# A gather kernel's first adapter, first activations and last output: found, turned and stored another way

## The chip, the cores and the metric

The kernel runs on one core of one Trainium2 chip. The metric is device time in microseconds (us), the median of the runs. TensorE is called PE, VectorE DVE, ScalarE ACT, GpSimd POOL and SyncE SP, as in the profile.

## The reference

128 samples of 64 x 1024 floats pass two layers, each with a residual. Layer one picks one of 16 matrices of 64 x 64 by a sample's index, layer two one of 8 adapters of 1024 x 1024. The inputs draw the second index from 3 to 7, so five adapters are used.

```python
def _L0_cond_ref(x, weights, condition):
    W = weights[condition]
    return jnp.einsum('bct,bcd->bdt', x, W)
def _L1_cond_ref(x, weight, adapter_ids):
    w = weight[adapter_ids]
    return jnp.einsum('bsi,boi->bso', x, w)
x = x + _L0_cond_ref(x, L0_cond_weights, itok_B_0_15)
x = x + _L1_cond_ref(x, L1_cond_weight, itok_B_3_7)
```

## The kernel before

**The arithmetic.** The identity is added to every matrix, so that the residuals come with the products. With x as 64 rows, z = x times the adapter turned over (the big product), and y = the small matrix times z. Each float operand is split in two float32r parts, hi (a copy) and lo (what is left), and a product is hi x hi, lo x hi and hi x lo.

**Slots.** Samples are sorted by adapter on the chip, and two samples of one adapter make a slot of 128 rows; where a group has an odd count, its last slot holds one. DVE works out a table (a row per slot: samples, how many to store, group, small matrices, chunks), which one DMA moves to one partition (`slot_row`, line 329), where every engine looks fields up (`look`, lines 188 to 195). `groups_ready` tells that POOL has made `group_row`, the adapters in order of their groups (lines 257 to 272).

**Order in a slot.** PE makes the first half of z (`sum_z`, lines 421 to 434, 24 matmuls of 512 columns in a slot of two samples), then y of the slot before (`sum_y`, 6 matmuls), then the second half of z. ACT copies out the hi parts, DVE makes the lo parts, ACT copies y out of PSUM and stores it on its own DMA queue (`store_y`). SP issues all loads. The next adapter comes in chunks during the slots and is turned by DVE; loops run over pairs of slots. There are 66 slots here (line 536 runs 66 times for each of two banks).

**The start.** Before slot 0 all of the first adapter is needed: 8 chunks of 128 x 1024. Chunk c is loaded by SP (`load_first`), gets its identity from POOL (`add_1_to_first`, line 254), is turned by PE in 8 transposes into a pair of PSUM banks (line 411; three pairs in turn), and is kept as hi by ACT (line 511) and lo by DVE (line 691). Chunks 6 and 7 land in the buffers of chunks 0 and 1, once these are turned. x of slot 0 comes in 8 small DMAs (line 343), is turned by DVE in 32 x 32 blocks (line 715), and split (lines 524, 724). POOL adds the identity to the small matrices too (line 275), for ACT and DVE to split (lines 506, 754).

**The end.** After the last z there is nothing left to overlap with: ACT keeps z's second half as hi (536), DVE makes its lo (740), PE sums y (444 to 446), ACT copies it out (541) and stores it (548).

The order of each engine's work is the order in which its block is written; semaphores hold it back. Some waits that matter here are:

```python
sp.wait_ge(groups_ready, 1)
first_ad = sp.value_load(group_row[0:1, 0:1], min_val=0, max_val=NAD - 1)
...
pool.wait_ge(table_moved, 16)
```

Of the kernel before, what the change touches and what calls it, by code (L numbers as in the profile page):

```python
# [5 lines left out]
P = 128  # L6
# [12 lines left out]
def conditional_residual_kernel(nc, x, cond_ids, adapter_ids, cond_w, adapter_w, out):  # L19
# [29 lines left out]
    x_quarters = x.rearrange("n (b r) (a m) -> n a r b m", a=BLOCKS, r=BLOCK)  # L49
    out_rows = out.rearrange("b c t -> (b c) t")  # L50
# [4 lines left out]
    with ExitStack() as ctx:  # L55
# [40 lines left out]

# [30 lines left out]
        group_id = sb("group_id", [1, NAD])  # L128
        group_row = sb("group_row", [1, NAD], I32)
# [23 lines left out]
        x_loaded = [sem(f"x_loaded{h}") for h in range(2)]  # L153
        first_loaded = [sem(f"first_loaded{c}") for c in range(CHUNKS_PER_GROUP)]
# [22 lines left out]
        y_made = sem("y_made")  # L177
        all_done = sem("all_done")
# [40 lines left out]

        block = ctx.enter_context(nc.Block())  # L220
# [5 lines left out]
        def _(pool):  # L226
# [23 lines left out]
            def add_1_to_first(c):  # L250
# [5 lines left out]

            pool.wait_ge(groups_made, 1)
# [48 lines left out]
        def _(sp):  # L306
# [18 lines left out]
            for c in range(2):  # L325
                load_first(c)
# [3 lines left out]
            for c in range(2, 5):  # L330
                load_first(c)
# [54 lines left out]

            for h in range(2):
# [6 lines left out]
        def _(pe):  # L394
# [74 lines left out]
            for c in range(CHUNKS_PER_GROUP):  # L469
                turn_first(c)  # L470
# [332 lines left out]
```

## Time and profile before

| | |
|---|---|
| median of 3 runs | 835.26 us (834.72 to 836.27) |
| the profiled execution | 834.99 us |
| its span | 833.2 us |
| PE busy | 808.3 us, 97% of the span |
| DVE, ACT, POOL busy | 449.6, 280.6, 27.4 us |
| moved over the span | 90.87 MB, mean 109 GB/s |

The profile shows one execution. Busy time is the time in which an engine had an instruction under way; an average over the span says nothing about a short stage at one end of it. A timeline row gives start, duration, engine, source line, what is written and read, how often (x), and in brackets how long the engine had been idle and what released it. SPq and ACTq are the DMA issues of SP and ACT.

### The profile page before, as it was taken

The numbers are of one execution on the slowest core, as the hardware profiler recorded it, in microseconds if no ns is written. First come the engines' busy times: TensorE is split into PE (matmuls) and PEld (weight loads), VectorE is DVE, ScalarE is ACT, GpSimd is POOL, SyncE is SP. The second block draws the span as 40 slices with busy tenths as digits, with TensorE's granted clock in tenths as the row PEclk, the third lists the DMA queues.
The fourth block names the chain that finished last, engine by engine and source line by source line (L and its number), as shares of the span: only waits on it lengthen the run. The fifth ranks groups of instructions, "written<-read, shape, count | busy, mean of one in ns | idle before, by whom it ended". The sixth has DMA issues, their size and how long they took to land.

```text
span 833.2 us, 17872 instructions
## 1 busy us (share of the span) xinstructions
PE 808.3 (97%) x3572; PEld 668.5 (80%) x3573; DVE 449.6 (54%) x466; ACT 280.6 (34%) x515; POOL 27.4 (3%) x61
## 2 busy tenths in 40 slices
PE   3899999999999999999999999999999999999996
PEld 2688888888888888888888888888888888888885
DVE  5756676466665434676663466665443344344432
ACT  2423334342433223333432333333332332232232
POOL 3000000000000000000000000000000000000000
PEclk9899999999999999999999999999999999999999
DMA  4544443444433324444332434433332232233232
GB/s 140 167 125 134 144 140 85 121 123 147 123 104 101 88 72 126 130 142 126 110 101 81 121 122 142 134 102 91 97 100 67 76 101 79 72 101 90 74 88 76
DMA packets 74271, 90.87 MB, mean 109 GB/s; under 512 B 13844, under 2 KB 65044, under 8 KB 74260
## 3 DMA queue, kind: packets, MB, share of 16 engines
q1 hardware_dynamic: 64020, 57.19, 22.3%
q10 hardware_dynamic: 10240, 33.56, 15.3%
q8 instruction: 4, 0.07, 0.0%
q14 instruction: 7, 0.06, 0.0%
HBM read 57.15 MB, written 33.55 MB: 109 GB/s over the span
## 4 chain that ended last, share of the span: by engine, by line
PE 96%; DMA 1%; DVE 1%; issue 1%; SPq 1%; ACTq 0%; POOL 0%; POOLq 0%; ACT 0%; DVEq 0%
PE z_ps L431 14%; PE first_ps L431 14%; PE z_ps L430 14%; PE first_ps L430 14%; PE z_ps L433 14%; PE first_ps L433 13%; PE y_ps L445 4%; PE y_ps L446 4%; PE y_ps L444 4%; DMA w_nat<-in_L_cond_weight_dram 1%; SPq L343 0%; DMA slot_row<-table_i 0%; DMA ids_i<-in_itok_B_dram 0%; PE first_ps L411 0%; ACTq L192 0%
## 5 line engine op out<-in xcount | busy, mean ns | idle before, releaser
L430 PE MATMUL z_ps<-w_hi,xt_hi 128*128 (+1 forms) x528 | 205.5, 389 | 0.0
L431 PE MATMUL z_ps<-w_lo,xt_hi 128*128 (+1 forms) x528 | 205.4, 389 | 0.0
L430 PE MATMUL first_ps<-w_hi,xt_hi 128*128 x528 | 205.4, 389 | 0.0
L431 PE MATMUL first_ps<-w_lo,xt_hi 128*128 x528 | 205.4, 389 | 0.0
L433 PE MATMUL z_ps<-w_hi,xt_lo 128*128 (+1 forms) x512 | 199.2, 389 | 0.0
L433 PE MATMUL first_ps<-w_hi,xt_lo 128*128 x480 | 186.7, 389 | 0.0
L715 DVE STREAM_TRANSPOSE x_turned<-x_in 128x1024 f32<-128x1024 f32 x67 | 143.6, 2143 | 23.9 <-issue 19.5
L524 ACT ACTIVATE xt_hi<-x_turned 128x1024 fp32r<-128x1024 f32 x67 | 71.1, 1061 | 227.7 <-DVE x_turned L715 227.7
L724 DVE TENSOR_TENSOR xt_lo<-x_turned,xt_hi 128x1024 fp32r<-128x1024 f32 x62 | 76.1, 1228 | 77.8 <-ACT xt_hi L524 77.8
L430 PEld LDWEIGHTS z_ps<-w_hi,xt_hi 128*128 128x128 f32 x528 | 99.2, 188 | 20.9
L430 PEld LDWEIGHTS first_ps<-w_hi,xt_hi 128*128 128x128 f32 x528 | 99.1, 188 | 20.8
L431 PEld LDWEIGHTS first_ps<-w_lo,xt_hi 128*128 128x128 f32 x528 | 99.1, 188 | 20.6
L431 PEld LDWEIGHTS z_ps<-w_lo,xt_hi 128*128 128x128 f32 x528 | 99.1, 188 | 20.5
L433 PEld LDWEIGHTS z_ps<-w_hi,xt_lo 128*128 128x128 f32 x512 | 96.1, 188 | 19.8
L433 PEld LDWEIGHTS first_ps<-w_hi,xt_lo 128*128 128x128 f32 x480 | 90.1, 188 | 18.5
L740 DVE TENSOR_TENSOR z_lo<-first_ps,z_hi 128x512 fp32r<-128x512 f32 x66 | 45.5, 689 | 94.8 <-ACT z_hi L536 94.5
L740 DVE TENSOR_TENSOR z_lo<-z_ps,z_hi 128x512 fp32r<-128x512 f32 x66 | 45.5, 689 | 92.4 <-ACT z_hi L536 91.0
L710 DVE TENSOR_TENSOR w_lo<-w_turned,w_hi x32 | 39.4, 1232 | 69.9 <-ACT w_hi L520 69.9
L520 ACT ACTIVATE w_hi<-w_turned x32 | 34.0, 1062 | 122.2 <-DVE w_turned L700 122.2
L541 ACT ACTIVATE y<-y_ps 128x512 f32<-128x512 f32 x132 | 71.3, 597 | 2.1 <-PE y_ps L446 2.1
L536 ACT ACTIVATE z_hi<-first_ps 128x512 fp32r<-128x512 f32 x66 | 39.1, 592 | 90.8 <-PE first_ps L433 66.2
L536 ACT ACTIVATE z_hi<-z_ps 128x512 fp32r<-128x512 f32 x66 | 39.1, 592 | 88.5 <-PE z_ps L433 70.9
(119 smaller groups left out, 444.0 us busy)
## 6 DMA issues: line engine op xcount, KB each, us to landing
x_in<-in_x_dram SPq DMA_DIRECT2D x544, 64.0 KB, 2.0
out_dram<-y ACTq DMA_DIRECT2D x128, 256.0 KB, 3.1
w_nat<-in_L_cond_weight_dram SPq DMA_DIRECT2D x128, 128.0 KB
w_nat<-in_L_cond_weight_dram SPq DMA_DIRECT2D x4, 512.0 KB, 4.3
w_turned<-in_L_cond_weight_dram SPq DMA_DIRECT2D x2, 512.0 KB, 3.8
y<-in_L_cond_weight_dram SPq DMA_DIRECT2D x2, 512.0 KB, 5.1
x_turned<-in_L_cond_weights_dram SPq DMA_DIRECT2D x2, 256.0 KB, 3.9
ids_i<-in_itok_B_dram SPq DMA_DIRECT2D x2, 0.5 KB, 2.1
```

The costliest lines, as they stand in the source:

```text
L430: nc.tensor.matmul(to, xt_hi[h][:, t, :], whi, start=(t == 0), stop=False)
L431: mm = nc.tensor.matmul(to, xt_hi[h][:, t, :], wlo, start=False, stop=last and not pair)
L433: mm = nc.tensor.matmul(to, xt_lo[h][:, t, :], whi, start=False, stop=last)
L444: nc.tensor.matmul(to, w0_slot[:, 0], z_hi[:, n], start=True, stop=False)
L520: nc.scalar.activation(of_chunk(w_hi, k), turned(k), ACT.Copy).then_inc(chunk_hi_made, 1)
L524: nc.scalar.activation(xt_hi[h][:], x_turned[h][:], ACT.Copy).then_inc(xt_hi_made, 1)
L536: nc.scalar.activation(z_hi[:, n], z_banks[h][n][:], ACT.Copy).then_inc(z_hi_made, 1)
L541: nc.scalar.activation(y[h][:, n * HALF:(n + 1) * HALF], y_ps[n][:], ACT.Copy).then_inc(y_made, 1)
L710: nc.vector.tensor_tensor(of_chunk(w_lo, k), turned(k), of_chunk(w_hi, k).bitcast(F32), ALU.subtract).then_inc(chunk_lo_made, 1)
L715: nc.vector.transpose(x_turned[h][:].rearrange("p t (b m) -> p b t m", m=BLOCK), x_in[h][:].rearrange("p (b m t) -> p b t m", b=BLOCKS, m= ...
L724: nc.vector.tensor_tensor(xt_lo[h][:], x_turned[h][:], xt_hi[h][:].bitcast(F32), ALU.subtract).then_inc(xt_lo_made, 1)
L740: nc.vector.tensor_tensor(z_lo[:, n], z_banks[h][n][:], z_hi[:, n].bitcast(F32), ALU.subtract).then_inc(z_lo_made, 1)
```

## The change

- **The first adapter.** DVE multiplies a countdown 8, 7, ..., 1 with "this adapter is used", takes the largest value and subtracts it from 8: the number of the first adapter used, right after the counts are known. SP waits for that (`first_known`) in place of `groups_ready`, and issues six chunks at once, then the table's DMA. The making of `group_row` moves back, to DVE behind the table and to POOL between chunks 3 and 4.
- **x of slot 0.** SP reads the two samples from the table's first row where DVE made it, and loads each with one DMA of 64 x 1024, behind six chunks and the table. PE turns it between chunks 3 and 4, ACT and DVE split it out of PSUM. Chunks 6 and 7 come behind it.
- **The small matrices** get their identity from DVE, ahead of its wait for `gathered`; their lo part is made behind all of the adapter.
- **The last y.** PE takes z_lo last in each half. ACT copies the left half of y, DVE the right one, and SP and ACT each store one sample in two halves of 512 columns.
- **Stores of the other slots** are issued by ACT ahead of the copy of z's second half (`keep_z_hi(s, h, 1)`), where they stood behind it.

```diff
+    x_rows = x.rearrange("b c t -> (b c) t")
...
+        X0 = "x of slot 0"
+        TURN_ORDER = [0, 1, 2, 3, X0, 4, 5, 6, 7]
+        TURN_OF = {what: i for i, what in enumerate(TURN_ORDER)}
+        FOR_FIRST_HALF = 5
...
+        def store_last(eng, k, pairs_past):
+            s = 2 * pairs_past + 1
+            *samples, stores = look(eng, s, SAMPLE_A, SAMPLE_B, STORES)
+            rows = slice(k * C, (k + 1) * C)
+            to = out_rows[bass.ds(samples[k] * C, C), :]
+            with eng.If(stores > k):
+                eng.wait_ge(y_made, 4 * pairs_past + 3)
+                eng.dma_start(to[:, 0:HALF], y[1][rows, 0:HALF]).then_inc(last_stored, 16)
+                eng.wait_ge(last_half_made, 1)
+                eng.dma_start(to[:, HALF:T], y[1][rows, HALF:T]).then_inc(last_stored, 16)
+            with eng.Else():
+                eng.sem_inc(last_stored, 32)
...
+            for c in range(3):
+                add_1_to_first(c)
+            pool.wait_ge(table_moved, 16)
+            nc.gpsimd.tensor_copy(slot_row[:, 1:LOOKED_UP + 1, CHUNKS_BEFORE], slot_row[:, 0:LOOKED_UP, CHUNKS]
+                                  ).then_inc(table_ready, 1)
+            add_1_to_first(3)
...
-            pool.wait_ge(w0_loaded, 2 * 16)
-            nc.gpsimd.tensor_tensor(w0_nat, w0_nat,
-                                    two_ident[:].rearrange("p (n d) -> p n d", n=1).to_broadcast([P, NCOND, C]),
-                                    ALU.add).then_inc(w0_with_1, 1)
-            for c in range(2):
-                add_1_to_first(c)
-            pool.wait_ge(table_moved, 16)
-            nc.gpsimd.tensor_copy(slot_row[:, 1:LOOKED_UP + 1, CHUNKS_BEFORE], slot_row[:, 0:LOOKED_UP, CHUNKS]
-                                  ).then_inc(table_ready, 1)
-            for c in range(2, CHUNKS_PER_GROUP):
+            for c in range(4, CHUNKS_PER_GROUP):
...
-            sp.wait_ge(groups_ready, 1)
-            first_ad = sp.value_load(group_row[0:1, 0:1], min_val=0, max_val=NAD - 1)
+            sp.wait_ge(first_known, 1)
+            first_ad = sp.value_load(first_row[0:1, 0:1], min_val=0, max_val=NAD - 1)
             def load_first(c):
                 if c >= OWN_PLACE:
-                    sp.wait_ge(first_turned, NH * (c - OWN_PLACE) + NH)
+                    sp.wait_ge(first_turned, NH * TURN_OF[c - OWN_PLACE] + NH)
                 sp.dma_start(first_nat[c], adapter_rows[bass.ds((first_ad * CHUNKS_PER_GROUP + c) * P, P), :]
                              ).then_inc(first_loaded[c], 16)
-            for c in range(2):
+            for c in range(6):
                 load_first(c)
             sp.wait_ge(table_made, 1)
             sp.dma_start(slot_row[:, 1:LOOKED_UP + 1, :], table_i[0:LOOKED_UP]).then_inc(table_moved, 16)
-            for c in range(2, 5):
+            _, first_samples = nc.values_load_multi_w_load_instructions(
+                table_i[0:1, SAMPLE_A:SAMPLE_B + 1], engines=[sp.engine], min_val=0, max_val=B - 1,
+                skip_runtime_bounds_check_because="the table is made on the chip, of clipped indices")
+            for k, sample in enumerate(first_samples):
+                sp.dma_start(x_in[0][k * C:(k + 1) * C, :], x_rows[bass.ds(sample * C, C), :]).then_inc(x0_loaded, 16)
+            for c in range(6, CHUNKS_PER_GROUP):
...
-            load_x(0, 0)
-            for c in range(5, CHUNKS_PER_GROUP):
-                load_first(c)
             load_x(1, 1)
-            sp.wait_ge(first_turned, NH * CHUNKS_PER_GROUP)
+            sp.wait_ge(groups_ready, 1)
+            sp.wait_ge(first_turned, NH * len(TURN_ORDER))
+            sp.sem_inc(x_loaded[0], PER_X)
...
+            store_last(sp, 0, pairs_past)
...
-            def turn_first(c):
-                pe.wait_ge(first_with_1, c + 1)
+            def turn_first(i):
+                if TURN_ORDER[i] == X0:
+                    pe.wait_ge(x0_loaded, 32)
+                    nat = x_in[0][:]
+                else:
+                    pe.wait_ge(first_with_1, TURN_ORDER[i] + 1)
+                    nat = first_nat[TURN_ORDER[i]]
...
-                pe.wait_ge(xt_lo_made, 1)
-                pe.wait_ge(first_lo_made, NH * TPB)
+                pe.wait_ge(first_lo_made, NH * FOR_FIRST_HALF)
...
-                sum_y(2 * pairs_past + 1, pair)
+                s = 2 * pairs_past + 1
+                for k in range(2):
+                    pe.wait_ge(w0_placed[k], s + 1)
+                w0_slot, rows = (w0_parts, P) if pair else (w0_twice, C)
+                for n in range(NH):
+                    to = y_ps[n][0:rows]
+                    pe.wait_ge(z_hi_made, NH * s + n + 1)
+                    nc.tensor.matmul(to, w0_slot[:, 0], z_hi[:, n], start=True, stop=False)
+                    nc.tensor.matmul(to, w0_slot[:, 1], z_hi[:, n], start=False, stop=False)
+                    pe.wait_ge(z_lo_made, NH * s + n + 1)
+                    nc.tensor.matmul(to, w0_slot[:, 0], z_lo[:, n], start=False, stop=True).then_inc(y_summed, 1)
...
                 place_w0_a(s)
+                store_y(before, 1 - h)
                 keep_z_hi(s, h, 1)
-                store_y(before, 1 - h)
-            for c in range(4):
-                keep_first_hi(c)
-            keep_xt_hi(0, 0)
-            for c in range(4, CHUNKS_PER_GROUP):
-                keep_first_hi(c)
+            for i in range(len(TURN_ORDER)):
+                keep_first_hi(i)
+            act.sem_inc(xt_hi_made, 1)
...
-            make_y(2 * pairs_past + 1, 1)
-            store_y(2 * pairs_past + 1, 1)
+            act.wait_ge(y_summed, 4 * pairs_past + 3)
+            nc.scalar.activation(y[1][:, 0:HALF], y_ps[0][:], ACT.Copy).then_inc(y_made, 1)
+            store_last(act, 1, pairs_past)
...
+            nc.vector.tensor_scalar(countdown[:], col_i[0:1, 0:NAD], -1.0, float(NAD), ALU.mult, ALU.add)
...
+            link(nc.vector.tensor_scalar(cnt[:, 1, :], counts_ps, 1.0, None, ALU.min))
+            link(nc.vector.tensor_tensor(countdown_used[:], countdown[:], cnt[0:1, 1, :], ALU.mult))
+            link(nc.vector.tensor_reduce(first_from_end[:], countdown_used[:], AX_X, ALU.max))
+            nc.vector.tensor_scalar(first_row[:], first_from_end[:], -1.0, float(NAD), ALU.mult, ALU.add
+                                    ).then_inc(first_known, 1)
             nc.vector.tensor_copy(looked[:, 0, :], ranks_ps)
-            nc.vector.tensor_scalar(cnt[:, 1, :], counts_ps, 1.0, None, ALU.min)
...
+            dve.wait_ge(w0_loaded, 2 * 16)
+            nc.vector.tensor_tensor(w0_nat, w0_nat,
+                                    two_ident[:].rearrange("p (n d) -> p n d", n=1).to_broadcast([P, NCOND, C]),
+                                    ALU.add).then_inc(w0_with_1, 1)
...
+            def keep_x0_lo(i):
+                def keep(samples, to):
+                    for n in range(NH):
+                        at = (slice(None), slice(n * TPB, (n + 1) * TPB), samples)
+                        turned_x = first_banks[i % TURNS][n][:].rearrange("p (t m) -> p t m", t=TPB)[:, :, samples]
+                        dve.wait_ge(first_hi_made, NH * i + n + 1)
+                        nc.vector.tensor_tensor(to[at], turned_x, xt_hi[0][at].bitcast(F32),
+                                                ALU.subtract).then_inc(first_lo_made, 1)
+                stores, = look(dve, 0, STORES)
+                with dve.If(stores > 1):
+                    keep(slice(0, P), xt_lo[0])
+                with dve.Else():
+                    keep(slice(C, P), xt_hi[0])
...
+            for i in range(TURN_OF[X0]):
+                keep_first_lo(i)
+            dve.wait_ge(table_ready, 1)
+            keep_x0_lo(TURN_OF[X0])
+            for i in range(TURN_OF[X0] + 1, len(TURN_ORDER)):
+                keep_first_lo(i)
             dve.wait_ge(w0_hi_made, 1)
             nc.vector.tensor_tensor(w0_all[:, 1], w0_nat, w0_all[:, 0].bitcast(F32), ALU.subtract).then_inc(w0_lo_made, 1)
-            for c in range(4):
-                keep_first_lo(c)
             dve.wait_ge(w0_zeroed, 1)
-            dve.wait_ge(table_ready, 1)
-            turn_x(0, 0)
-            keep_xt_lo(0, 0)
-            for c in range(4, CHUNKS_PER_GROUP):
-                keep_first_lo(c)
-            dve.wait_ge(first_lo_made, NH * CHUNKS_PER_GROUP)
+            dve.wait_ge(first_lo_made, NH * len(TURN_ORDER))
+            dve.sem_inc(x_is_turned, 1)
+            dve.sem_inc(xt_lo_made, 1)
...
+            dve.wait_ge(y_stored[1], 32 * pairs_past + STORED_AHEAD)
+            dve.wait_ge(y_summed, 4 * pairs_past + 4)
+            nc.vector.tensor_copy(y[1][:, HALF:T], y_ps[1][:]).then_inc(last_half_made, 1)
```

POOL's order, from its first wait for data on. `first_loaded` is a chunk's landing, `table_moved` the table's, `groups_made` DVE's part of the groups. Before:

```order
L258 TENSOR_TENSOR used_id<-cnt,col 1x8 [waits groups_made,consts_made]
L260 TENSOR_TENSOR is_group<-is_group,used_id 1x64 [waits pool_step]
L265 TENSOR_TENSOR half_id<-is_group 1x32 [waits pool_step]
L267 TENSOR_TENSOR quarter_id<-half_id 1x16 [waits pool_step]
L269 TENSOR_TENSOR group_id<-quarter_id 1x8 [waits pool_step]
L272 CAST group_row<-group_id 1x8 [waits pool_step]
L275 TENSOR_TENSOR x_turned<-x_turned,two_ident 128x1024 [waits w0_loaded]
L254 TENSOR_TENSOR w_nat<-w_nat,ident 128x128 [waits first_loaded0]
L254 TENSOR_TENSOR w_nat<-w_nat,ident 128x128 [waits first_loaded1]
L282 COPY slot_row<-slot_row 1x70 [waits table_moved]
L254 TENSOR_TENSOR w_turned<-w_turned,ident 128x128 [waits first_loaded2]
```

Now:

```order
L282 TENSOR_TENSOR w_nat<-w_nat,ident 128x128 [waits first_loaded0,consts_made]
L282 TENSOR_TENSOR w_nat<-w_nat,ident 128x128 [waits first_loaded1]
L282 TENSOR_TENSOR w_turned<-w_turned,ident 128x128 [waits first_loaded2]
L288 COPY slot_row<-slot_row 1x70 [waits table_moved]
L282 TENSOR_TENSOR w_turned<-w_turned,ident 128x128 [waits first_loaded3]
L293 TENSOR_TENSOR used_id<-cnt,col 1x8 [waits groups_made]
L295 TENSOR_TENSOR is_group<-is_group,used_id 1x64 [waits pool_step]
L300 TENSOR_TENSOR half_id<-is_group 1x32 [waits pool_step]
L302 TENSOR_TENSOR quarter_id<-half_id 1x16 [waits pool_step]
L304 TENSOR_TENSOR group_id<-quarter_id 1x8 [waits pool_step]
L307 CAST group_row<-group_id 1x8 [waits pool_step]
L282 TENSOR_TENSOR y<-y,ident 128x128 [waits first_loaded4]
```

Chunk 3 now stands behind the wait for the table, and chunk 4 behind the six small operations of the groups as well.

SP's order. The wait that each of its loads inherits is the last one ahead of it. Before:

```order
L316 TENSOR_LOAD group_row [waits groups_ready]
L316 ISA x2
L322 ISA
L322 DMA w_nat<-in_L_cond_weight_dram 128x1024
L322 ISA
L322 DMA w_nat<-in_L_cond_weight_dram 128x1024
L329 DMA slot_row<-table_i 1x70x8 [waits table_made]
L322 ISA
L322 DMA w_turned<-in_L_cond_weight_dram 128x1024
```

Now, from the fifth chunk on (the load of `first_row`, which waits for `first_known`, stands ahead of the first):

```order
L347 DMA y<-in_L_cond_weight_dram 128x1024
L347 ISA
L347 DMA y<-in_L_cond_weight_dram 128x1024
L354 DMA slot_row<-table_i 1x70x8 [waits table_made]
L355 TENSOR_LOAD table_i
L359 ISA
L359 DMA x_in<-in_x_dram 64x1024
L359 ISA
L359 DMA x_in<-in_x_dram 64x1024
L347 ISA [waits first_turned]
L347 DMA w_nat<-in_L_cond_weight_dram 128x1024
```

Six chunks of 512 KB (the two on `y` are the last) are ahead of the table in SP's queue, where two were.

## Rows read from the trace of the kernel before

**Rows 1.** The page: busy us, share of the span and instructions of each engine.
```profile
PE 808.3 (97%) x3572; PEld 668.5 (80%) x3573; DVE 449.6 (54%) x466; ACT 280.6 (34%) x515; POOL 27.4 (3%) x61
```

**Rows 2.** Waits of PE from 35 to 833 us: in total, times, longest.
```profile
PE y_ps L444 <- DVE z_lo L740: 0.7, 1, 0.7
```

**Rows 3.** Timeline of 0 to 62 us, DVE, POOL and SP up to the table.
```profile
6.80 0.17 DVE L631 TENSOR_SCALAR pairs_i<-pairs_i 128x8 int32<-128x8 int32 x1
7.00 0.17 DVE L632 CAST cnt<-pairs_i 128x8 f32<-128x8 int32 x1
...
8.62 0.19 POOL L258 TENSOR_TENSOR used_id<-cnt,col 1x8 f32<-1x8 f32 x1 [5.91 <-DVE is_group L642]
...
10.19 0.18 POOL L272 CAST group_row<-group_id 1x8 int32<-1x8 f32 x1
...
11.18 0.16 DVE L663 COPY got<-z_ps 128x5 f32<-128x5 f32 x1 [1.11 <-PE z_ps L403]
...
11.40 0.91 SPq L322 DMA_DIRECT2D w_nat<-in_L_cond_weight_dram  x2
...
11.64 1.06 DVE L667 TENSOR_SCALAR fill<-got,absent 128x2 f32<-128x2 f32 x1
...
14.16 0.17 DVE L685 CAST table_i<-table 128x8 int32<-128x8 f32 x1
14.24 1.22 DVE L754 TENSOR_TENSOR w_all<-x_turned,w_all 128x1024 fp32r<-128x1024 f32 x1
14.36 0.98 SPq L329 DMA_DIRECT2D slot_row<-table_i  x1
```

**Rows 4.** The same timeline: the turning of the first adapter.
```profile
15.83 3.49 PE L411 MATMUL first_ps<-ident,w_nat 128*128 128x128 f32 x16 [4.68 <-POOL w_nat L254]
15.99 0.46 POOL L254 TENSOR_TENSOR w_nat<-w_nat,ident 128x128 f32<-128x128 f32 x1 [0.22 <-DMA w_nat<-in_L_cond_weight_dram]
...
16.67 0.30 POOL L282 COPY slot_row<-slot_row 1x70 int32<-1x70 int32 x1 [0.23 <-DMA slot_row<-table_i]
...
19.42 1.16 PE L411 MATMUL y_ps<-ident,w_turned 128*128 128x128 f32 x8
...
22.34 1.29 DVE L691 TENSOR_TENSOR w_lo<-first_ps,w_hi 128x512 fp32r<-128x512 f32 x2 [0.26 <-ACT w_hi L511]
...
26.79 1.97 PE L411 MATMUL y_ps<-ident,y 128*128 128x128 f32 x8 [1.95 <-POOL y L254]
...
32.53 0.53 PE L430 MATMUL z_ps<-w_hi,xt_hi 128*128 128x512 f32 x1
```

**Rows 5.** Stretches: length, busy of each engine, granted clock, DMA share, GB/s.
```profile
13.00:15.00 2.00, 0.00 (x0) 0.00 (x0) 1.83 (x13) 0.76 (x1) 0.32 (x1) 1.00 1.04 414
...
26.00:32.00 6.00, 4.78 (x21) 4.38 (x22) 4.88 (x7) 4.09 (x7) 1.36 (x3) 0.50 0.72 221
```

**Rows 6.** DMA issues from 11.3 to 11.8 us (chunk 0): KB, us to landing.
```profile
w_nat<-in_L_cond_weight_dram SPq DMA_DIRECT2D x1, 512.0 KB, 3.2
```

**Rows 7.** Timeline of 822 to 834 us: from the last z to the last store.
```profile
824.94 0.60 ACT L536 ACTIVATE z_hi<-first_ps 128x512 fp32r<-128x512 f32 x1 [4.08 <-PE first_ps L433]
...
825.57 0.69 DVE L740 TENSOR_TENSOR z_lo<-first_ps,z_hi 128x512 fp32r<-128x512 f32 x1 [5.08 <-ACT z_hi L536]
825.99 1.13 ACTq L548 DMA_DIRECT2D out_dram<-y  x2
...
826.66 0.40 PE L445 MATMUL y_ps<-z_lo,w_parts 128*128 128x512 f32 x1
...
826.89 0.39 PE L446 MATMUL y_ps<-z_hi,w_parts 128*128 128x512 f32 x1
827.62 1.09 ACT L541 ACTIVATE y<-y_ps 128x512 f32<-128x512 f32 x2 [2.08 <-PE y_ps L446]
829.20 1.13 ACTq L548 DMA_DIRECT2D out_dram<-y  x2
```

**Rows 8.** Waits of ACT from 35 to 824 us, in slots of one sample.
```profile
ACT z_hi L536 <- PE first_ps L431: 5.7, 3, 1.9
```

More of the change, by code:

```diff
@@ L128, in conditional_residual_kernel @@
         group_id = sb("group_id", [1, NAD])
+        countdown = sb("countdown", [1, NAD])
+        countdown_used = sb("countdown_used", [1, NAD])
+        first_from_end = sb("first_from_end", [1, 1])
+        first_row = sb("first_row", [1, 1], I32)
         group_row = sb("group_row", [1, NAD], I32)
@@ L153, in conditional_residual_kernel @@
         x_loaded = [sem(f"x_loaded{h}") for h in range(2)]
+        first_known = sem("first_known")
+        x0_loaded = sem("x0_loaded")
         first_loaded = [sem(f"first_loaded{c}") for c in range(CHUNKS_PER_GROUP)]
@@ L177, in conditional_residual_kernel @@
         y_made = sem("y_made")
+        last_half_made = sem("last_half_made")
+        last_stored = sem("last_stored")
         all_done = sem("all_done")
@@ L389, in _ @@
                 sp.sem_inc(all_done, 1)
-                sp.wait_ge(y_stored[h], 32 * pairs_past + 32 + STORED_AHEAD)
+                sp.wait_ge(y_stored[h], 32 * pairs_past + (STORED_AHEAD if h else 32 + STORED_AHEAD))
                 sp.sem_inc(all_done, 1)
+            sp.wait_ge(last_stored, 64)
+            sp.sem_inc(all_done, 1)
         @block.tensor
@@ L467, in slot @@
                 for_both(stores, lambda pair: sum_z(h, 1, buf, pair))
-            for c in range(CHUNKS_PER_GROUP):
-                turn_first(c)
+            for i in range(len(TURN_ORDER)):
+                turn_first(i)
             pe.wait_ge(table_ready, 1)
@@ L506, in _, with keep_first_hi @@
             nc.scalar.activation(w0_all[:, 0], w0_nat, ACT.Copy).then_inc(w0_hi_made, 1)
-            def keep_first_hi(c):
+            def keep_first_hi(i):
+                what = TURN_ORDER[i]
                 for n in range(NH):
-                    act.wait_ge(first_turned, NH * c + n + 1)
-                    nc.scalar.activation(w_hi[:, 0, n * TPB:(n + 1) * TPB, c * P:(c + 1) * P],
-                                         first_banks[c % TURNS][n][:].rearrange("p (t m) -> p t m", t=TPB),
+                    tiles = slice(n * TPB, (n + 1) * TPB)
+                    to = xt_hi[0][:, tiles] if what == X0 else w_hi[:, 0, tiles, what * P:(what + 1) * P]
+                    act.wait_ge(first_turned, NH * i + n + 1)
+                    nc.scalar.activation(to, first_banks[i % TURNS][n][:].rearrange("p (t m) -> p t m", t=TPB),
                                          ACT.Copy).then_inc(first_hi_made, 1)
@@ L576, in slot @@
                 place_w0_a(s)
+                store_y(before, 1 - h)
                 keep_z_hi(s, h, 1)
-                store_y(before, 1 - h)
-            for c in range(4):
-                keep_first_hi(c)
-            keep_xt_hi(0, 0)
-            for c in range(4, CHUNKS_PER_GROUP):
-                keep_first_hi(c)
+            for i in range(len(TURN_ORDER)):
+                keep_first_hi(i)
+            act.sem_inc(xt_hi_made, 1)
             keep_xt_hi(1, 1)
@@ L641, in _ @@
             link(nc.vector.tensor_tensor(looked[:, 1:3, :], src[:], cnt[:], ALU.subtract))
-            nc.vector.tensor_tensor(is_group[:], looked[0:1, 2:3, :].to_broadcast([1, NAD, NAD]),
-                                    col[0:1, 0:NAD].rearrange("p (g u) -> p g u", u=1).to_broadcast([1, NAD, NAD]),
-                                    ALU.is_equal).then_inc(groups_made, 1)
             link(nc.vector.tensor_scalar(pair_count[:, 0:1], src[0:1, 0, NAD - 1:NAD], -1.0, None, ALU.add))
```

20 lines of the change are left out of this document (12 added, 8 removed).

## The prediction

> **What bounds the kernel now.** I read the page first. PE is busy in 97% of the span [rows 1], so the reader is to see that little can be won in the middle. The waits of PE from 35 us on say it outright: one wait of 0.7 us in 798 us [rows 2], and that one is in the last y. The change takes no matmul away. So its worth is the start, up to the first z matmul at 32.53 us [rows 4], and the end, from the last z at 824.94 to the span's end at 833.2 us [rows 7]. I then read the timeline of both, and ask what released each step.
>
> At the start the chain goes from `group_row` (ready at 10.37) to SP's first chunk at 11.40, 1.03 later [rows 3]; chunk 0 lands 3.2 us after its issue [rows 6]; x and three more chunks are issued only after the table has landed, which is at about 16.6, when POOL copies it [rows 4]. At the end, ACT is still issuing the stores of the slot before at 825.99 to 827.12, so it starts on the last y at 827.62, though PE's last two sums began at 826.66 and 826.89, 0.23 apart; the last two stores go out at 829.20 to 830.33 [rows 7].
>
> **First adapter.** The two steps of a linked pair on DVE are 0.20 us apart [rows 3]. The counts are read two such steps and a bit ahead of the 6.80 row, at about 6.45. Three links and the last operation make `first_row` by 6.45 + 4 x 0.20 = 7.25, and the countdown adds 0.07 ahead of it: 7.3. With the same 1.03, SP issues chunk 0 at **8.3 in place of 11.4**. It lands 3.2 later, at 11.5. While two chunks streamed alone the core moved 414 GB/s [rows 5], so a chunk of 0.524 MB takes 1.27; I take 1.3. Issues are 0.55 apart (two in 0.91), so they don't bind. Six chunks have landed by 11.5 + 5 x 1.3 = **18.0**.
>
> **The table.** It was ready at 14.33 [rows 3]. Ahead of it come the countdown and three links (+0.7); `is_group` leaves (-0.15). The addition to the small matrices, 1.22 like the DVE operation of that shape, stands where DVE idled 1.11 [rows 3]: +0.15. As POOL no longer does it, the 1.06 of `fill`, against 0.16 or so for its neighbours, should go (-0.9). POOL's additions to chunks 0 and 1 (0.46 each [rows 4]) may block some of the small operations, as one held up `fill`: 0 to +0.9. I take **14.2**. The table's DMA took 14.36 to about 16.6, 2.3. Bounds for its landing, M: flowing past the chunks, 14.2 + 2.3 = 16.5; behind all six on the same queue, 18.0 or a little later. The row we have had only one chunk in flight ahead and can't tell. I take **M = 18.0**: chunk 0 landed at 14.6, and POOL had to wait for chunk 1 until 15.99 [rows 4], 1.4 later, though issued 0.55 later, so loads of one queue were served one after the other at the stream's pace.
>
> The Trainium skill (DMA: Bandwidth & Descriptors, Queues, rings and completion order) says that on each DMA engine descriptors are consumed in ring order. By it M is 18.0, without it 16.5; the trace of before does not decide between them.
>
> **POOL.** This is where the order matters. Chunk 3 waits for the table: copy 0.30, addition 0.46, and small gaps, so PE may turn it at M + 0.95 = 18.95. The six operations of the groups took 8.62 to 10.37, 1.75 [rows 3], so chunk 4 is free at M + 3.2 = 21.2. PE turns chunk 3 and x in between, so this costs nothing; if both were turned at full speed it would cost 0.0 to 0.1.
>
> **PE.** After M come six turns: chunk 3, x, chunks 4 to 7. Bounds: 6 x 1.16 = 7.0 and 6 x 1.97 = 11.8. The first two chunks after 4.68 us of idleness took 3.49, 1.75 each, though the clock's row says 1.00, and the next took 1.16 [rows 4]. In the new order PE has some 1.9 us with nothing between chunk 2 (12.3 + 3.5 + 1.2 = 17.0) and chunk 3. I take two turns at 1.75 and four at 1.16, 8.1, nearest to what followed a wait here. The first z comes at 18.95 + 8.1 + 0.1 = **27.2**. Covers: chunk 7 is issued near 17.5 behind x and chunk 6, and lands at 18.0 + 3 x 1.3 = 21.9, before PE gets to it at 26; if the DMAs lagged by over 3 us, it would bind. DVE makes the lo parts at 1.29 per chunk [rows 4], slower than PE's 1.16, but three pairs of banks give it slack, and the first half of z wants only five of the nine. x of slot 1 is split well before PE gets to it, 11 us after the first z: its transpose (2.1), hi and lo follow DVE's last lo part near 28. At zero, too: the 32 x 32 turning of x of slot 0 leaves DVE.
>
> Before, z began at 32.53 with its first matmuls still slowed (0.53 for the first); at full pace that is 32.7. **Start: 32.7 - 27.2 = 5.5 us won.**
>
> **End.** Offsets from 824.94. ACT's hi takes 0.60, DVE's lo ends at 826.26 [rows 7]. PE made three matmuls behind it, 0.23 apart; now two are made before, so the sum is ready 0.46 sooner, near 826.8. DVE copies the right half: no row has this copy, so it is bounded by 0.60 (ACT's) and 0.69 (DVE's two-input form), 827.5. ACT's left half runs at 825.6, since the older stores are gone from there. The second halves are issued on both queues at about 827.6; before, the last of two stores was issued at 829.85 and the span ended 3.35 later. A store of 128 KB takes between the table's 2.3 and those 3.35 of a 256 KB one; with four in flight I take 3.0. End 830.6 against 833.2: **2.6 won** (bounds 1.9 and 3.3).
>
> **Stores moved ahead of the second hi copy.** ACT was idle 4.08 us ahead of it in a slot of two samples [rows 7], and in the slots of one sample up to 1.9 [rows 8]; two issues take 1.13, and the lookup ahead of them some 0.45 (825.54 to 825.99 [rows 7]), 1.6. The cover is ACT's idle time, and behind it the first half of the next z, since PE wants that copy only for y. Cost: 0.
>
> **The sum.** 834.99 - 5.5 - 2.6 = **826.9 us**, made against the profiled execution; the median of the runs is 0.27 higher, and a measurement can tell about 0.2% (1.7 us) from no change.
>
> **Rivals.**
> - *The table isn't held back.* M = 16.5, all else the same: 825.4. Then chunk 3 isn't late, and PE's gap shrinks to a few tenths, which favours the full pace too (824.2). For it: the table is 2.2 KB, and its DMA kept 2.3 us with a chunk in flight. Against: six chunks, not one. 12%.
> - *The clock falls.* PE's gap ahead of chunk 3 comes after a thin stage, and in the trace the clock went to 0.50 after a stretch of short bursts. Then six turns take 11.8 and z starts at 30.9, so 1.8 is won at the start and 2.6 at the end: 830.6. Against: PE turned chunk 2 at 1.16 after such bursts. 15%. The Trainium skill (TensorE: Matmul & The Clock Gate, Part 4) says that transposes don't count as PE activity like matmuls. By that rule this rival would hold for certain; the 1.16 at a granted 1.00 speaks against it.
> - *The end gives half.* DMAs of 2 KB rows, or the completion of four stores, take as long as before: 828.2. 9%.
> - *The moved stores bite, slower than before.* If ACT's copy of z's second half came late enough for PE to wait in y, each of the 66 slots would pay. It decides from 8.1 / 66 = 0.12 us a slot; with a third of ACT's 0.60, 0.2, the time is 840.1, as 66 x 0.2 = 13.2. Against it: PE needs the copy only after 24 (or 16) matmuls at 0.23, 3.7 us or more. 2%.
> - *The start does not do what it says*, since something else (DVE's lo parts, a chunk's landing) sets the first z near 30: 829.7. 5%.
>
> My forecast has the other 57%. **Range.** The low end takes the first rival at full pace with the better end, 823.6; the high end the clock's fall, 831.0. Faster than 0.2%: 0.95; same 0.03 (two of the rivals together); slower 0.02.
>
> **What would show it.** SP's first chunk at about 8.3; six landings 1.3 apart; `slot_row` copied by POOL at 18.0 (at 16.5 the first rival); chunk 3 turned at 19; six turns to 27.1, by their durations 1.16, 1.75 or 1.97 and the granted clock; the first z at 27.2; PE without waits from there on; and at the end the DVE copy, four half stores, and 5.7 us from the last z to the end of the span in place of 8.3. A first z after 30, or a PE wait in y in every slot, would make the prediction wrong.

## The result, and the profile after

The changed kernel takes 845.95 us (median of 4, 842.65 to 847.82) against 834.99 for the kernel before, a ratio of 1.0124 with a 95% interval of 1.009 to 1.0159. It is 11 us slower where I had forecast 8 us faster. The profiled execution took 846.66 us with a span of 844.9. Of all executions reported here one, of e10, took 1672 us, twice the usual time; it is left out of its ratio.

I divide the span by two marks, which every table below uses: the first z matmul of PE, and the start of ACT's last z_hi copy.

| | start: to the first z | middle: first z to last z_hi | end: to the span's end | span |
|---|---|---|---|---|
| before | 32.53 | 792.41 | 8.27 | 833.2 |
| after | 30.33 | 808.85 | 5.72 | 844.9 |
| difference | -2.20 | **+16.44** | -2.55 | +11.7 |

The page of the changed kernel, busy us by engine and then the chain that ended last, answers to [rows 1]:

```profile
PE 817.0 (97%) x3580; PEld 667.4 (79%) x3581; DVE 449.7 (53%) x472; ACT 280.1 (33%) x515; POOL 22.2 (3%) x60
...
PE 43%; DVE 17%; ACTq 11%; issue 9%; ACT 8%; DVEq 5%; SPq 1%; DMA 1%; POOL 0%; POOLq 0%
```

The first line still says 97% for PE and would mislead: a matmul is recorded with 0.39 us though matmuls follow each other every 0.23 us, so a short wait hides in it. The second line is the one to read. In the kernel before PE held 96% of that chain; now PE has 43%, DVE, ACT and their queues have 41%, and 9% is "issue", time in which the engine that the chain follows waited for nothing that the profile shows. The waits of PE from 35 to 840 us (in total, times, longest), where [rows 2] had a single one:

```profile
PE y_ps L481 <- DVE z_lo L813: 6.7, 15, 0.5
PE y_ps L481 <- DVE w_parts L809: 1.9, 4, 1.1
PE z_ps L467 <- DVE xt_lo L797: 0.5, 1, 0.5
```

They add up to 9.1 of the 16.44 us; these rows don't show the rest.

Where they come from is seen in a slot that brings a chunk. First the kernel before, ACT's timeline in one such slot (start, duration, engine, line, operation; in brackets how long ACT was idle ahead of it and until what), then DVE's:

```profile
65.04 1.06 ACT L520 ACTIVATE w_hi<-w_turned  x1 [3.83 <-DVE w_turned L700]
66.01 0.57 ACT L536 ACTIVATE z_hi<-z_ps 128x512 fp32r<-128x512 f32 x1
66.48 1.08 ACT L541 ACTIVATE y<-y_ps 128x512 f32<-128x512 f32 x2
67.44 0.32 ACT L531 ACTIVATE w_twice<-w_all 128x128 fp32r x1
67.64 0.30 ACT L532 ACTIVATE w_parts<-w_all 64x128 fp32r x1
68.25 0.60 ACT L536 ACTIVATE z_hi<-z_ps 128x512 fp32r<-128x512 f32 x1 [0.31 <-PE z_ps L433]
69.31 1.15 ACTq L548 DMA_DIRECT2D out_dram<-y  x2
```

```profile
68.56 0.23 DVE L736 CAST w_parts<-w_all 64x128 fp32r x1
68.88 0.69 DVE L740 TENSOR_TENSOR z_lo<-z_ps,z_hi 128x512 fp32r<-128x512 f32 x1
69.68 2.15 DVE L715 STREAM_TRANSPOSE x_turned<-x_in 128x1024 f32<-128x1024 f32 x1
```

ACT is idle only **0.31 us** ahead of the second z_hi copy, not 4.08 as in [rows 7] or 1.9 as in [rows 8]: `w_hi`, the copy of the turned chunk, comes late in the slot and pushes all that is behind it. In the first sixteen slots with a chunk this idle time was never above 0.86 us. The same slot after the change, ACT and then DVE:

```profile
66.05 1.08 ACT L589 ACTIVATE y<-y_ps 128x512 f32<-128x512 f32 x2
67.00 0.32 ACT L579 ACTIVATE w_twice<-w_all 128x128 fp32r x1
67.20 0.30 ACT L580 ACTIVATE w_parts<-w_all 64x128 fp32r x1
67.30 1.15 ACTq L596 DMA_DIRECT2D out_dram<-y  x2
68.72 0.60 ACT L584 ACTIVATE z_hi<-z_ps 128x512 fp32r<-128x512 f32 x1 [1.21 <-issue]
```

```profile
68.12 0.22 DVE L809 CAST w_parts<-w_all 64x128 fp32r x1
69.35 0.69 DVE L813 TENSOR_TENSOR z_lo<-z_ps,z_hi 128x512 fp32r<-128x512 f32 x1 [1.00 <-ACT z_hi L584]
70.36 2.15 DVE L788 STREAM_TRANSPOSE x_turned<-x_in 128x1024 f32<-128x1024 f32 x1 [0.32 <-issue]
```

The stores take ACT 1.21 us between `w_parts` and z_hi. DVE, which went straight from `w_parts` to `z_lo` before, now waits 1.00 for it, and behind `z_lo` stands the transpose of the next x, with which the next slot's chain begins: x_turned (DVE), xt_hi (ACT), xt_lo and the chunk's transpose (DVE), w_hi, z_hi, y and `w_parts` (ACT), z_hi again, z_lo (DVE). Every step waits for the one ahead of it, on the same engine or the other. In the kernel before this ring just kept up with PE's work of a slot of two samples (successive chunk transposes from 50.07 to 135.29 us, seven intervals of 12.17 on average; ACT's second z_hi copies are 12.24 apart, 56.01 and 68.25, and both waited some 0.3 us for PE). After, the same seven intervals run from 48.48 to 139.80, 13.05 each: 0.88 longer, close to the 1.21 of the stores less the 0.31 that was idle. There are 32 such transposes, in four runs of eight slots; over each run's seven intervals the ring takes 6 to 7.5 us longer than before. A part of that is made up between the runs, where the gap is 1.5 to 3.5 us shorter than before, and PE loses the rest: 16.44 / 4 = 4.1 us a run.

At the start, PE's turning and POOL's copy of the table, which answer to [rows 4]; SP's first chunk went out at 8.26:

```profile
12.25 3.93 PE L448 MATMUL first_ps<-ident,w_nat 128*128 128x128 f32 x16 [0.67 <-POOL w_nat L282]
16.77 1.97 PE L448 MATMUL y_ps<-ident,w_turned 128*128 128x128 f32 x8 [0.58 <-POOL w_turned L282]
22.74 1.97 PE L448 MATMUL first_ps<-ident,w_turned 128*128 128x128 f32 x8 [4.00 <-POOL w_turned L282]
24.50 1.91 PE L448 MATMUL first_ps<-ident,x_in 128*128 128x128 f32 x8
26.21 1.68 PE L448 MATMUL y_ps<-ident,y 128*128 128x128 f32 x8
27.73 1.05 PE L448 MATMUL first_ps<-ident,y 128*128 128x128 f32 x8
...
30.33 0.47 PE L467 MATMUL z_ps<-w_hi,xt_hi 128*128 128x512 f32 x1
```

```profile
21.98 0.30 POOL L288 COPY slot_row<-slot_row 1x70 int32<-1x70 int32 x1 [5.27 <-DMA slot_row<-table_i]
```

The table was issued at 14.21 but reached POOL only at 21.98, and PE stood 4.00 us for the chunk behind it. The end, answering to [rows 7]:

```profile
839.18 0.60 ACT L584 ACTIVATE z_hi<-first_ps 128x512 fp32r<-128x512 f32 x1 [4.08 <-PE first_ps L470]
...
839.86 0.60 ACT L644 ACTIVATE y<-y_ps 128x512 f32<-128x512 f32 x1
...
841.09 0.69 DVE L853 COPY y<-y_ps 128x512 f32<-128x512 f32 x1 [0.59 <-PE y_ps L542]
841.95 0.50 ACTq L244 DMA_DIRECT2D out_dram<-y  x1
841.98 0.53 SPq L244 DMA_DIRECT2D out_dram<-y  x1
```

### The profile page after: what moved, and what is told of

Same layout as the page of the kernel before. It is cut to its first block, busy times and chain, and to the rows that moved or that the text cites. A ratio compares the mean times of both kernels' runs of the same rounds, so it can differ in the third digit from the quotient of the medians.

```text
span 844.9 us, 17894 instructions
## 1 busy us (share of the span) xinstructions
PE 817.0 (97%) x3580; PEld 667.4 (79%) x3581; DVE 449.7 (53%) x472; ACT 280.1 (33%) x515; POOL 22.2 (3%) x60
## 4 chain that ended last, share of the span: by engine, by line
PE 43%; DVE 17%; ACTq 11%; issue 9%; ACT 8%; DVEq 5%; SPq 1%; DMA 1%; POOL 0%; POOLq 0%
DVE x_turned L788 8%; DVE w_turned L773 8%; PE z_ps L467 7%; PE z_ps L468 7%; PE z_ps L470 6%; PE first_ps L468 6%; PE first_ps L467 6%; PE first_ps L470 5%; ACTq L206 4%; ACTq L596 4%; ACT xt_hi L572 4%; DVEq L206 3%; ACT z_hi L584 3%; PE y_ps L481 2%; PE y_ps L482 2%
```

## The experiments

All twelve, with the three stretches of one profiled execution of each. Ratios are to the kernel before, run on the same chip beside them.

| run | start | middle | end | median us | ratio |
|---|---|---|---|---|---|
| e1 stores back | 30.66 | 795.43 | 7.5 | 835.03 | 0.9996 (0.9985 to 1.0008) |
| e2 stores moved alone | 31.86 | 807.78 | 7.5 | 848.87 | 1.0151 (1.0123 to 1.0178) |
| e3 stores by slot | 28.94 | 796.66 | 5.7 | 833.13 | 0.9978 (0.9966 to 0.9989) |
| e4 table by ACT | 30.18 | 796.57 | 5.8 | 834.47 | 0.9989 (0.9977 to 1.0001) |
| e5 place behind | 29.60 | 792.38 | 5.7 | 829.89 | 0.9944 (0.9927 to 0.9961) |
| e6 end alone | 32.45 | 792.55 | 5.7 | 831.93 | 0.9971 (0.996 to 0.9983) |
| e7 four ahead | 28.04 | 795.21 | 5.8 | 832.05 | 0.9967 (0.9954 to 0.9979) |
| e8 ACT padded | 30.77 | 794.67 | 5.8 | 833.72 | 0.9985 (0.9976 to 0.9995) |
| e9 first store ahead | 29.58 | 794.14 | 5.7 | 830.46 | 0.9937 (0.9925 to 0.995) |
| e10 behind and four | 29.36 | 792.39 | 5.8 | 829.02 | 0.9921 (0.9907 to 0.9934) |
| e11 and w0_lo early | 29.63 | 792.37 | 5.7 | 827.83 | 0.9918 (0.9903 to 0.9934) |
| e12 late start, behind | 31.75 | 792.38 | 5.8 | 832.17 | 0.9969 (0.9958 to 0.998) |

### Whether the moved stores cost the middle (e1, e2, e3)

e1 takes the move of the stores out of the changed kernel, e2 puts that move alone into the kernel before. The edit of e1, in `slot` on ACT (e2 is the reverse, in the other kernel):

```diff
                 place_w0_a(s)
-                store_y(before, 1 - h)
                 keep_z_hi(s, h, 1)
+                store_y(before, 1 - h)
```

> The changed kernel with the stores put back behind the second hi copy; all else as changed. Theory A (in slots with a chunk, ACT and DVE form one chain as long as the slot, and the two store issues now stand in it): the 16.4 us lost between the first and the last z come back, the start keeps its 2.2, the end gives about 1 since ACT again issues older stores first; 831.8 us, no PE wait in y in the middle. Rival B (the earlier start or the new order of loads makes later chunks or x late): stays near 845.

> The kernel before with nothing changed but the stores moved ahead of the second hi copy. Theory A: first to last z grows from 792.4 to about 808.8 us, so 851 us. Rival B: within 1 us of 835.

e2 was slower by 14 us, and its middle (807.78) is within 1.1 us of the changed kernel's. e1's middle fell by 13.4 of the 16.4. So the move alone makes the slowdown; theory A holds, and the rival, that it lay in the rest of the change, is out. One thing didn't fit: e1's middle was 795.43, not 792.4, and so its time 835.03, not 831.8. Its end of 7.5 is near what was expected: the older stores stood again ahead of ACT's half of the last y (827.14 to 828.27, with the y copy at 828.75), so the move is needed there. e3 therefore puts it in by slot:

```diff
                 place_w0_a(s)
-                store_y(before, 1 - h)
-                keep_z_hi(s, h, 1)
+                with act.If(last > first):
+                    keep_z_hi(s, h, 1)
+                    store_y(before, 1 - h)
+                with act.Else():
+                    store_y(before, 1 - h)
+                    keep_z_hi(s, h, 1)
```

> The changed kernel, but in the 32 slots that bring in a chunk the stores stand behind the second hi copy, in the others ahead of it. Theory A: only slots with a chunk pay, so nothing is lost in the middle and the end keeps its 2.5: 830.2 us. Rival C (a store issued earlier costs in every slot, by its data's collision with the loads): the 34 other slots keep their half of the loss, 838.

It is faster than both kernels, and rival C, which wanted 838, is out: with the stores ahead in all other slots, e3's middle is 1.2 us from e1's, so the loss of the move sat in the chunk slots. But it was 3 us slower than the 830.2 expected, again in the middle.

### The late table (e4, e7)

e4 has ACT issue the table's DMA on its own queue, behind its copies of chunk 0, in place of SP:

```diff
-            sp.dma_start(slot_row[:, 1:LOOKED_UP + 1, :], table_i[0:LOOKED_UP]).then_inc(table_moved, 16)
...
-            for i in range(len(TURN_ORDER)):
+            keep_first_hi(0)
+            act.wait_ge(table_made, 1)
+            act.dma_start(slot_row[:, 1:LOOKED_UP + 1, :], table_i[0:LOOKED_UP]).then_inc(table_moved, 16)
+            for i in range(1, len(TURN_ORDER)):
                 keep_first_hi(i)
```

> As the kernel with the stores by slot, and the table's DMA is issued by ACT (behind the copies of chunk 0), so on the other queue, not behind six chunks. Theory D (the table landed at 21.9 because it stood behind the chunks in SP's queue): it lands near 17.2, chunk 3 is turned at 18.8, and the first z comes 2 to 3 us earlier than at 30.3: 827.5 us. Rival E (the DMA engines are shared, so a table issued into that traffic lands late on any queue): table near 21, 830.

```profile
14.11 1.40 ACTq L633 DMA_DIRECT2D slot_row<-table_i  x1
```

```profile
22.68 0.30 POOL L288 COPY slot_row<-slot_row 1x70 int32<-1x70 int32 x1 [6.58 <-DMA slot_row<-table_i]
```

Both rows are e4's. The table went out at 14.11 with an empty queue of its own and landed no earlier than behind six chunks on SP's. Rival E was right on the table, though the time came out 4.5 us above its 830. So the table was not held by its place in SP's queue. That the loads in flight hold it on either queue is what remains, and e7 tests it. The ring order that I cited from the Trainium skill (DMA: Bandwidth & Descriptors, Queues, rings and completion order) speaks of one queue's descriptors on an engine; this run shows that leaving that ring brings nothing here. e7 puts fewer loads ahead:

```diff
-            for c in range(6):
+            for c in range(4):
                 load_first(c)
...
-            for c in range(6, CHUNKS_PER_GROUP):
+            for c in range(4, CHUNKS_PER_GROUP):
                 load_first(c)
```

> The kernel of e3 with four chunks issued ahead of the table's move instead of six (then table, x of slot 0, the other four). Theory H (the table and x landed late because of what was issued ahead of them, whatever the queue): POOL's copy of the table begins at 18 to 19 instead of 21.2, the first z at 27.5 instead of 28.9. By theory F little of it reaches the end: 832.5 to 833. Rival: the table lands as late as before (21 to 22.7), since its packets are slow for another reason.

```profile
17.80 0.30 POOL L288 COPY slot_row<-slot_row 1x70 int32<-1x70 int32 x1 [0.95 <-DMA slot_row<-table_i]
```

With four chunks ahead the table reaches POOL at 17.80, 3.4 us earlier than in e3. e10 and e11, which have the same edit, show 16.99 and 17.83, and all seven executions with six ahead 20.89 or later, so theory H holds for the table. For the first z it isn't shown: 28.04 in e7, but 29.36 and 29.63 in e10 and e11, and 28.94 to 30.77 in the six kernels with six ahead on SP's queue (after, e1, e3, e5, e8, e9). The median is 1.1 below e3's, as expected, but the intervals of the ratios overlap.

### Where the earlier start goes (e5, e6, e12)

In e1, e3 and e4 a start 2 to 3.6 us earlier came with a middle 3 to 4 us longer. The start scatters from one execution to the next, with the same code for it, and the end of the middle did not follow: in e1, e3 and e8 the first z came at 30.66, 28.94 and 30.77, and the last z_hi copy at 826.09, 825.60 and 825.44. So something else than PE's start set it. e5 takes 0.5 us off the ring of each chunk slot:

```diff
-                place_w0_a(s)
                 with act.If(last > first):
                     keep_z_hi(s, h, 1)
+                    place_w0_a(s)
                     store_y(before, 1 - h)
                 with act.Else():
+                    place_w0_a(s)
                     store_y(before, 1 - h)
                     keep_z_hi(s, h, 1)
```

e6 is the kernel before with only the new end and e3's stores by slot.

> The kernel of e3 with the two copies of place_w0_a put behind the second z_hi copy in slots that bring a chunk. e3 measured 833.13, its first z came 3.6 us earlier than before, and 796.7 us lay between the first z and the last against 792.4 before. Theory F (in chunk slots the DVE-ACT chain has next to no slack, so a start that is earlier, or one long issue on ACT, is not made up for many slots): with about 0.5 us more slack in each chunk slot the middle falls to 793 to 794, the time to 830 to 831. Rival G (the middle's 4 us are lost elsewhere, on PE or in transfers): no change, 833.

> The kernel before with the change's end (last y in halves) and the stores ordered by slot as in e3, the start left as it was. Theory F: the start change gives what its earlier first z gives only where the chain has slack, so here the middle is 792.4 as before, the end 5.7, the time 832.4, as good as e3 with its first z 3.6 us later. Rival G (the earlier start is worth its 2 to 3.6 us, and e3's long middle comes from the stores or the end part): 835 or more with a middle of 796.

Both came out as theory F has it. e6, with its first z 3.5 us later than e3's, is no slower (831.93 against 833.13, intervals of the ratios overlapping): in the order of e3 the new start was worth nothing. e5's middle is back at 792.38, and PE waits for nothing from 28 us to the last z. The chain of e5 that ended last:

```profile
PE 97%; DMA 1%; DVE 1%; issue 0%; POOL 0%; SPq 0%; DVEq 0%
```

e12 closes the square: e6 with the edit of e5.

> The kernel of e6 (old start, new end, stores by slot) with place_w0_a behind the second z_hi copy in chunk slots, as e5 has it. Theory F: with the old start PE already runs through the middle in 792.4, so the extra slack of the chain brings nothing: middle 792.4, time 831.9 as e6. Then the start change is worth what e11 gains over this one, some 3 to 4 us, and only with that slack. Rival M (place_w0_a behind is worth something by itself, whatever the start): 830 or less.

832.17, as e6, with the same middle. The shorter ring is worth nothing by itself, and the earlier start nothing in the order of e3; together they are worth 2.3 us (e12 against e5, by medians from two chips on which the kernel before took 834.93 and 834.65). That no execution of e5 was as slow as the fastest of e12 (830.86, 831.53) supports this, though the intervals of their ratios just touch. The next part shows a second way to let the start through.

### The long issue in slot 1 (e8, e9)

ACT's two first stores took 5.72 us to issue in e3, the first of them 5.06 where the median of all is 0.485 (ACT's timeline):

```profile
53.14 0.59 ACT L584 ACTIVATE z_hi<-first_ps 128x512 fp32r<-128x512 f32 x1
53.68 5.72 ACTq L596 DMA_DIRECT2D out_dram<-y  x2
61.01 1.06 ACT L572 ACTIVATE xt_hi<-x_turned 128x1024 fp32r<-128x1024 f32 x1 [7.28 <-issue]
```

In the kernel before the two took 1.61 at that place, and xt_hi followed at 60.15. So e3, which was 2.87 us ahead at this z_hi copy, left the slot behind. All that e3 loses on the ring stands in the first of the four runs of chunk slots: its seven intervals take 90.40 us against 85.22 before, the first alone 15.63 against 12.31, and the other three runs take 86.2 as before. e8 shifts ACT's code by 128 increments of an unused semaphore at its start, e9 lets the stores of slot 1 alone go ahead of z_hi:

```diff
+            for _ in range(128):
+                act.sem_inc(padded, 1)
             act.wait_ge(consts_made, CONSTS)
```

```diff
+                if stores_ahead:
+                    store_y(before, 1 - h)
+                    keep_z_hi(s, h, 1)
+                    return
                 with act.If(last > first):
...
-            slot(0, 1, 0)
+            slot(0, 1, 0, stores_ahead=True)
```

> The kernel of e3 with 128 semaphore increments on ACT at its very start, where ACT has nothing to do: no work is changed, only where ACT's code lies. In e3 ACT's first store took 5.06 us to issue, once, against 0.75 in the kernel before, with packets of the instruction queues in the same stretch. Theory I (ACT waited for its own code there): the long issue is gone from that line or stands at another, and if it falls into idle time the middle shortens by 1 to 2 us, the time to 831 to 832. Rival J (the store waits for something of the DMA queues): the first store takes 5 us again, the time 833.

> The kernel of e3, whose stores go ahead of the second z_hi copy in slot 1 alone among the slots with a chunk, where in the changed kernel the first store took 0.77 us to issue and in e3 5.06. Theory K (that one long issue of ACT in slot 1 is what ate e3's earlier start: its second z_hi copies lay 15.6 us apart there against 12.2): the two copies lie under 14 us apart, the middle is 794 to 795, the time 831 to 832. Rival L (the long issue only filled time in which the chain was waiting for chunks or DVE anyway): again over 15 us and 833.

In e8 the two stores took 5.53 again, at the same line. The Trainium skill (Runtime: NRT & Kernel Launch, Instruction fetch mechanics) says that a taken branch whose target lies outside the engine's window of code makes it wait for a fetch; if such a fetch were the cause, a change of where the code lies might have moved or ended the wait, and it did neither. But the padding shifts a branch and its target alike, so this run makes that cause less likely and doesn't exclude it. In e9 the wait was gone:

```profile
54.31 1.59 ACTq L596 DMA_DIRECT2D out_dram<-y  x2
56.11 0.60 ACT L584 ACTIVATE z_hi<-first_ps 128x512 fp32r<-128x512 f32 x1 [1.60 <-issue]
60.07 1.06 ACT L572 ACTIVATE xt_hi<-x_turned 128x1024 fp32r<-128x1024 f32 x1 [3.36 <-DVE x_turned L796]
```

Its second z_hi copies of slots 1 and 2 lie 11.7 us apart (56.11 and 67.79) against 15.6 in e3, the middle is 794.14 and the time 830.46: theory K. Against e6 (831.93, the ratios' intervals apart) this start is now worth 1.5 us, without e5's shorter ring. The long issue and the lack of slack thus cost together: e5 has the long issue too (4.57 for the two) and still a middle of 792.38. What makes the issue long is open. It was there in every kernel with the new start and the stores behind z_hi in slot 1 (e1, e3, e4, e5, e7, e8, e10, e11), and in none with the old start (before, e6, e12) or with the stores ahead (after, e2, e9). Whether SP began its eight x loads before or after it didn't decide: e5 (SP at 54.27, ACT at 54.82) has it and e9 (54.32 and 54.31) hasn't.

### Together (e10, e11)

e10 has the edits of e5 and e7. e11 moves DVE's w0_lo as well, from behind the first adapter's lo parts to behind the second chunk's:

```diff
             for i in range(TURN_OF[X0]):
                 keep_first_lo(i)
+                if i == 1:
+                    dve.wait_ge(w0_hi_made, 1)
+                    nc.vector.tensor_tensor(w0_all[:, 1], w0_nat, w0_all[:, 0].bitcast(F32),
+                                            ALU.subtract).then_inc(w0_lo_made, 1)
```

> e5 and e7 in one: place_w0_a and the stores behind the second z_hi copy in chunk slots, four chunks ahead of the table. e7 had its first z 0.9 us before e3's, and 1.6 before e5's own. Theory F: since e5's middle was 792.4, as long as before and with no wait of PE, the earlier first z goes through whole: first z 28.0, middle 792.4, time 828.3. Rival: the chain is the bound again at this earlier start: a middle of 794, the time 829.9 as e5.

> e10 with DVE's w0_lo (1.22 us) moved from behind the last lo part of the first adapter, ahead of the transpose of slot 1's x, into DVE's idle time before the fourth chunk. By theory F, if the chain still holds e10 back the middle gets shorter by up to 1.2 us and the time with it (to 827.5 or so); if e10's middle is 792.4 already, it changes nothing (828.3).

Both middles are at 792.4, so nothing is left for the ring to give, and e11's edit shows no gain beyond the scatter (0.9918 against 0.9921). e10's first z was at 29.36 in the profiled run, not 28.0: PE waited 1.29 us for chunk 4 and 0.32 for chunk 7, in e7 0.59 and nothing. At 827.8 to 829.0 us these two are faster than both kernels, and than the kernel before by 0.8%, close to the 1% that I had forecast for the change, but by other edits than the change had. Against e12, which has the old start, e11 gains 4.3 us by the medians, the worth of the start once it goes through.

## Why the prediction was wrong

**"Stores moved ahead of the second hi copy. ... Cost: 0."** This is the step that failed. The cover I named, ACT's idle time ahead of that copy, was read in the last slot [rows 7] and in the slots of one sample [rows 8], where no chunk is turned. I had looked at two kinds of slot out of three. In a chunk slot it was 0.31 us, and the stores took 1.2 in most of these slots and 1.6 in the first, as priced. The second cover, "PE wants that copy only for y", looked at one reader only; the other is DVE, which can't start the next x before it has made z_lo. The cost measured is 16.4 us in the changed kernel and 15.4 in e2.

**The rival on the other side** had the right edit and put its decision at 0.12 us a slot of 66; the measured 16.44 / 66 = 0.25. Its price was near by luck: it had every slot pay, and 32 did, 0.51 each. Its mechanism was half right: PE does wait in y, 6.7 us in 15 recorded waits, but for z_lo, which DVE makes from the late copy. I argued against it with PE's need of the copy, and gave it 2%. PE's single wait [rows 2] made me take the middle as safe. That row says that PE didn't wait. It doesn't say how much later the others could have been without a wait of PE, and here that was next to nothing.

**The start**: 5.5 us forecast, 2.2 measured. First issue at 8.3 (8.26), table ready at 14.2 (issued at 14.21) and the six turns after the table at 8.1 (22.74 to 30.33, 7.6) were right or near. M, the landing of the table, was the term that was off: 18.0 forecast, 21.98 measured, beyond both my bounds. I took 1.3 us a chunk from a stretch in which two chunks streamed; with six issued the landings were far slower than that (issue to landing 3.3 us for chunk 0 and 10.5 for chunk 5, so that the sixth was there near 21.4, not at 18.0). In windows of the changed kernel (length, busy of each engine, granted clock, DMA share, GB/s), what [rows 5] showed as 414 held for a short time only:

```profile
14.00:18.00 4.00, 3.42 (x16) 2.80 (x15) 2.96 (x6) 1.87 (x5) 0.61 (x2) 1.00 1.03 398
18.00:22.00 4.00, 0.74 (x4) 0.34 (x2) 1.38 (x2) 1.12 (x2) 0.02 (x1) 1.00 1.03 244
```

The second stretch has the DMA engines just as busy and moves 244 GB/s; it holds the landing of the table. The rival "the start does not do what it says", at 5%, describes this part. "The clock falls" didn't decide: four blocks of turns, three of them after the table, ran at 1.68 to 1.97 with a granted clock of 1.00 in the record, but the six after the table took 7.6, less than I had allowed.

And a start won is not a time won. Even with the stores put right, e3 gave nothing for its 3.6 us, which the prediction nowhere considered: the ring of DVE and ACT, with the one long store issue in slot 1, sets the pace there, and DVE's first x transpose in the middle came at 34.01 after against 34.40 before, though PE began 2.2 us earlier.

**The end**: 2.6 forecast, 2.55 measured (2.9 from the last issue at 841.98 to the span's end at 844.9, 3.0 taken). This term was right. Its stated lower bound of 1.9 doesn't follow from the terms: with 3.35 us for a store they give 2.25.

## What to carry to other kernels

An engine's idle time ahead of an operation is a cover only in the kind of slot in which it was read: list that row for every kind of slot the loop has, and take the smallest. When PE shows no waits, work out how far the other engines' own cycle (here transpose, copy, subtraction, over DVE and ACT) is from being the bound, before putting anything into it or expecting an earlier start to pass through it. For a small transfer behind a burst of large ones, what counted here was how many large loads had been issued ahead of it, not whose queue it was on.

## What the runs showed of the hardware

A 2.2 KB transfer took 2.3 us from its issue to POOL's use of it with two 512 KB loads ahead of it, 2.7 to 3.6 with four (e7, e10, e11), and 6.7 to 8.6 with six, on either queue (in e4 14.11 to 22.68 on ACT's). With DMA share near 1.0 in both, the core moved 398 GB/s in one 4 us stretch and 244 in the next.

Blocks of eight transposes took 1.05 to 1.16 us or 1.68 to 1.97 us, with the granted clock recorded as 1.00 in all of them in the changed kernel, so the record did not tell when PE ran slow there. In e1, e3, e4 and e5 it did: from 22 to 26 us, where blocks took up to 1.97, the granted clock was 0.50 to 0.57. The Trainium skill (TensorE: Matmul & The Clock Gate, Part 4) says that transposes don't count as PE activity like matmuls. The trace of the changed kernel does not agree: three blocks of transposes, at 27.73, 28.62 and 29.51, ran at 1.05 to 1.06 ahead of the first z matmul, after a stage of turnings alone.

Two store issues of ACT took 4.6 to 5.9 us together in slot 1 of eight kernels, where the same two took 1.58 to 1.61 in the other six; it came with the new start and the stores behind z_hi, never without both, and the cause is open.
